# Attention scores for the row maxima: 64 contraction rows instead of 128, heads in pairs, and no transfers that zero the other rows

## The reference, cut to what matters

```
q = apply_rope(proj(Wq))
k = apply_rope(proj(Wk))
v = proj(Wv)
scores = jnp.einsum('bhqd,bhkd->bhqk', q, k) / np.sqrt(HEAD_DIM)
scores = jnp.where(causal[None, None], scores, -jnp.inf)
attn = jax.nn.softmax(scores, axis=-1)
out = jnp.einsum('bhqk,bhkd->bhqd', attn, v)
```

## Time and profile before

| | |
|---|---|
| device time, three runs | 2914.5, 2906.5, 2914.12 us, median 2914.12 |
| the profiled execution, from its first to its last instruction | 2910.5 us |
| time outside that span | not listed for it alone; the median of the runs is 3.6 us above the span |
| PE busy | 2715.2 us, 93% |
| PE weight loads busy | 1717.6 us, 59% |
| DVE, ACT, POOL busy | 1671.6, 1068.5, 928.5 us |
| first attention | about 37 to 430 us of the span |
| in 56 to 430 us of the span: PE, DVE, ACT, POOL busy | 335.62, 254.85, 183.99, 79.54 us of 374.00 |

### The profile page before, as it was taken

One profiled execution on the slowest core, in us unless ns is written; L12 is line 12 of the kernel. 1 busy time (PEld: TensorE's weight loads), 2 busy tenths in 40 slices (PEclk: granted clock), 3 DMA queues, 4 the chain that ended last, 5 costly groups with the idle time before them and its releaser, 6 DMA issues. The chain is left out here.

```text
span 2910.5 us, 35472 instructions
## 1 busy us (share of the span) xinstructions
PE 2715.2 (93%) x13556; PEld 1717.6 (59%) x13556; DVE 1671.6 (57%) x3449; ACT 1068.5 (37%) x1953; POOL 928.5 (32%) x898
## 2 busy tenths in 40 slices
PE   7988989999999999999999999899999999849995
PEld 4445545564656655556555567556666666627983
DVE  6676661217576574575562227688888888433323
ACT  2543551114454453444452115234443444212221
POOL 3222210003232232232220016266666666640004
PEclk8999999989999999999999999899999999869996
DMA  5231301030000000000002000000000000341222
GB/s 181 59 85 46 85 6 59 1 123 20 1 1 1 1 1 1 1 1 1 15 1 101 0 29 1 12 16 12 16 12 16 12 16 16 123 173 39 71 63 87
DMA packets 55961, 108.98 MB, mean 37 GB/s; under 512 B 8128, under 2 KB 32832, under 8 KB 54640
## 3 DMA queue, kind: packets, MB, share of 16 engines
q1 hardware_dynamic: 52720, 98.32, 10.7%
q0 software_dynamic: 3072, 8.39, 0.9%
HBM read 71.10 MB, written 27.00 MB: 34 GB/s over the span
## 5 line engine op out<-in xcount | busy, mean ns | idle before, releaser
L1229 PE MATMUL ps<-back 128*128 128x512 f32 x576 | 292.0, 596 | 0.3 <-ACT back L1270 0.3
L1270 ACT ACTIVATE back<-ps 128x512 f32<-128x512 f32 x288 | 170.0, 597 | 266.4 <-PE ps L1220 264.7
L1265 ACT ACTIVATE back<-ps,front 128x128 f32<-128x128 f32 (+7 forms) x256 | 188.9, 738 | 77.1 <-DVE front L1310 75.3
L1220 PEld LDWEIGHTS ps<-front,back 128*128 128x128 f32 x1152 | 140.8, 141 | 118.2 <-issue 94.8
L1353 POOL TENSOR_TENSOR back<-back 128x512 f32<-128x512 f32 x72 | 91.4, 1269 | 359.5 <-DVE back L1298 359.3
L1363 POOL TENSOR_SCALAR back<-back,front 128x128 f32<-128x128 f32 (+5 forms) x192 | 142.4, 745 | 191.4 <-DVE front L1329 188.6
L1310 DVE TENSOR_REDUCE front<-ps 128x1 f32<-128x128 f32 (+7 forms) x256 | 194.0, 758 | 8.8
L809 ACT ACTIVATE back<-ps 128x1024 f32<-128x1024 f32 (+1 forms) x192 | 150.9, 810 | 128.8 <-PE ps L721 128.2
L1911 DVE TENSOR_TENSOR_SCAN back<-ps,back 128x512 f32<-128x512 f32 x128 | 155.6, 1217 | 43.8 <-PE ps L1728 43.8
L1220 PE MATMUL ps<-front,back 128*128 128x128 f32 x1152 | 170.5, 273 | 3.4 <-DVE back L1335 3.4
L1303 DVE TENSOR_TENSOR ps<-ps,front 128x128 f32<-128x128 f32 x256 | 76.0, 297 | 166.1 <-PE ps L1211 166.1
(11 more groups left out here) (305 smaller groups left out, 5810.5 us busy)
## 6 DMA issues: line engine op xcount, KB each, us to landing
whole<-l_w SPq DMA_DIRECT2D x32, 512.0 KB
front<-back SPq DMA_DIRECT2D x128, 64.0 KB, 2.0
rounded<-qh SPq DMA_DIRECT2D x28, 256.0 KB
rounded<-kh SPq DMA_DIRECT2D x56, 128.0 KB
xg<-front SPq DMA_DIRECT2D x1, 6016.0 KB, 31.8
front<-xg SPq DMA_DIRECT2D x47, 128.0 KB, 2.1
yg<-front SPq DMA_DIRECT2D x47, 128.0 KB, 1.7
front<-l_win SPq DMA_DIRECT2D x1, 4640.0 KB, 17.7
```

What stands on the lines that cost most here:

```text
L1220: t = e.transpose(p[:, h * 128:h * 128 + 128], self.P[n % 2][:, h, j * 128:j * 128 + 128], net.ident)
L1229: e.matmul(PS[:, 7, :], self.V[:, j, G % 4 * 128:G % 4 * 128 + 128], self.turned(("turn", n, j)), start=(j == 0), stop=(j == qt)).then_inc ...
L1265: e.activation(self.P[n % 2][:, h, :nk], s[:, :nk], ACT.Exp, bias=st[:, 0, h:h + 1], scale=1.0, accum_out=st[:, 1, h:h + 1]).then_inc(A.se ...
L1270: e.activation(self.turned(step), self.bank(step), ACT.Copy).then_inc(A.sem, 1)
```

## The change

The matmul of s1 reads only the 64 rows with data. Its steps come in pairs of heads with the same due time; the heads of a pair, 0 with 2 and 1 with 3, have their data in different halves of the rows. The transfers of a set are issued in the order 0, 2, 1, 3, and the ones that zeroed the two extra rows are left out; the count that a waiting matmul asks for falls from 64 to 48 for each set.

```
+    TURNS = (0, 2, 1, 3)
...
-        self.moved = [[net.flag("a_set%d_%d" % (i, h), 48 + 3 * 64) for h in range(4)] for i in range(2)]
+        self.moved = [[net.flag("a_set%d_%d" % (i, h), 48 + 3 * 48) for h in range(4)] for i in range(2)]
...
             if u == 0:
-                s1 = [(t, 0, h) for h in range(4) for t in range(4)]
+                s1 = [(t, 0, h) for a in range(2) for t in range(4) for h in (a, a + 2)]
             else:
-                s1 = [(t, r, h) for t in range(4) for r in range(q + 1) for h in range(4)]
+                s1 = [(t, r, h) for t in range(4) for r in range(q + 1) for h in self.TURNS]
             if pe or dve:
                 for n, s in enumerate(s1):
-                    add(at + reach * (n + 0.5) / len(s1), "s1", u, *s)
+                    add(at + reach * (2 * (n // 2) + 1.0) / len(s1), "s1", u, *s)
...
-            w.wait_ge(self.moved[z % 2][h], 48 + 64 * (z // 2))
+            w.wait_ge(self.moved[z % 2][h], 48 + 48 * (z // 2))
...
-                t = e.matmul(o[:, 0:n], self.QS[:, s, h, qt], self.KS[:, s, h, 512 * r:512 * r + n], start=True, stop=True)
+                rows = slice(64, 128) if h < 2 else slice(0, 64)
+                t = e.matmul(o[:, 0:n], self.QS[rows, s, h, qt], self.KS[rows, s, h, 512 * r:512 * r + n], start=True,
+                             stop=True)
...
-            for h in range(4):
+            for h in self.TURNS:
                 self.move(e, w, z, h, slice(0, 1024), self.moved[s][h])
-                q = self.QS[:, s, h, :].bitcast(F32)
-                e.dma_start(q[32 * h:32 * h + 2, :], q[32 * h + 2:32 * h + 4, :]).then_inc(self.moved[s][h].sem, 16)
```

## The result

The changed kernel takes 2954.71 us (median of four runs, 2941.83 to 2965.86), the kernel before 2914.31 us beside it (four runs, 2906.5 to 2923.2). The ratio is 1.0131, with a 95% interval of 1.0096 to 1.0167: 40 us slower, where 22 to 25 were forecast. The profiled execution is the slowest of the four, 2965.86 us with a span of 2964.1.

What follows compares the result with a forecast made beforehand. TensorE was taken to set the pace in the attention. From the 2910.5 us span, plus 48 for changes of form, minus 34 for overlap, plus 13 for banks, minus 2 swallowed, came 2936 us; range 2900 to 2968.

Steps and rivals of the forecast that it cites:

- 64 rows save nothing by themselves: In s1, a step of 64 rows streams as many columns as one of 128, so nothing is saved.
- Pairs run at once: In s1, the second step of each pair of heads costs nothing, saving 34 us.
- Changes of form, 0.19 us each: On TensorE, switching between 128-row and 64-row steps drains the array and exposes a weight load; 250 changes, 48 us.
- the same holds around pv: At pv's steps, changes of form lengthen the passages too: 0.33 for 0.23 us before, 0.34 for 0.23 behind.
- Banks, 13 us: At s1's three banks, steps wait for VectorE's reads: 9 us in runs of four, 4 after pairs; 0 to 22.
- Swallowed, 2 us: In the attention, some extra work goes into TensorE's 26 us of waits; 2 us taken off.
- the rival "swallowed": In the attention, TensorE's waits shrink as its stream grows: 0 to 8 us more, 2911 to 2919 us; chance 0.13.
- The clock, 0 us: Half-clock stretches, mostly at the turn of units, widen the range some 8 us either way; chance of deciding 0.02.
- The transfers: On SP's queue, 24 issues fewer and the new order count 0, bounds -1 and +2 us.
- the signs that the prediction named: In the timeline after: pair starts under 0.02 us apart, TensorE busy 15 to 25 us longer, s1 waits in runs of four.
- the pairs don't overlap: In s1, second steps save nothing, changes of form still cost 48 us: 2958 us; chance 0.18.
- Faster: At changes of form, a pair's weight load is hidden, 0.08 us per change or less, down to 2889.5 us; chance 0.17.

Runs made afterwards that it cites:

- e3: The kernel before with s1 reading only the 64 rows with data, in the old order, zeroing transfers kept; ratio to before 1.0271.
- e2: The changed kernel with heads 0 and 1, 2 and 3 as pairs, their data in the same half of the rows; ratio to before 1.0226.
- e1: The changed kernel with s1 reading all 128 rows again and the zeroing transfers back, order in pairs kept; ratio to before 1.0057.
- e4: The changed kernel with the 24 zeroing transfers put back and nothing else; ratio to before 1.0120.
- e6: The kernel before with two filling matmuls in each unit's wait for the maxima; ratio to before 0.9982.
- e5: e1 with an extra matmul of 64 rows and 32 columns ahead of each pair; ratio to before 1.0255.
- e11: The changed kernel with VectorE reading only the first 128 columns of every s1 result; ratio to before 1.0004.
- e10: e1 with VectorE reading only the first 128 columns of every s1 result; ratio to before 0.9871.
- e9: The kernel before with VectorE reading only the first 128 columns of every s1 result, for the maxima; ratio to before 0.9855.

## Why the prediction was right, and which of its steps were not

The direction, the main mechanism (changes of form cost more than overlap saves) and the range held. The size was off, 22 to 25 us forecast and 40 measured, and the step most at fault is one that the text set to nothing: "This widens the range by some 8 us either way and decides nothing". That the range held is luck in part: the saving by overlap was counted 12 us too high and the clock at least 23 us too low, but the banks 16 us too high or more, and these errors partly cancel. By its steps:

*64 rows save nothing by themselves.* Right, shown by e3: it is the slowest of all.

*Pairs run at once.* Right in kind, shown by e2 and by the rows above. Mis-sized: the sum counted all second steps, 34 us. 119 of 184 pairs overlap, which by the same prices is 34 x 119/184 = 22 us. The others wait for a bank that VectorE still reads (34.5 us in all, 62 of the 65 released by VectorE). The text had these waits, but added them to a full overlap, which they exclude.

*Changes of form, 0.19 us each.* The price is confirmed row by row (0.10 before, 0.42 instead of 0.23 for the pair, 0.11 behind it). 250 of them are 48 us. The sentence that the same holds around pv is not quite right: the earlier trace rows give 0.10 + 0.09 + 0.11 = 0.30 us for both changes, 0.15 each. Changes into and out of pv stay at 190 in number, so the sum is hardly touched.

*Banks, 13 us.* Mis-sized. s1 steps stand 22.6 us behind the stream after the change (by the count of e1, in which overlapping seconds have none), 25.2 before. The change adds waits through the pairs (e1: 33.7) and takes them away again through its slower issue: -3 us in all.

*Swallowed, 2 us.* The extra waits at s1 that vanish are in the line above. The waits at the maxima fell by 1.7 us, 13.9 to 12.2. Over all steps it was more: banks and swallowed together were put at +11 us, and the waits at full clock fell by 15. This is the mechanism of the rival "swallowed", beside the forecast's own and too small to cancel it.

*The clock, 0 us.* Wrong. Half clock rose by 68.8 us in the attention. At 0.33 us each (e4 against the changed kernel) that is 23 us; counted from all starts it is 31. I took the stretches for a matter of the waits at the maxima, whose number the change leaves alone. They are that in the kernel before (e6), but changes of form add to them (e5, and e11 against e10, where the waits are nearly gone).

The sum so becomes 48 - 22 - 3 + 23 = 46 us, against 43.7 between the last transposes of the maxima, and by the second table 28 - 15 + 31 = 44, where the forecast had 14 + 11 + 0 = 25. For e11 against e10 it is 48 - 26 - 5 + 20 = 37, against 39.1. The rate of 0.33 is from one pair of profiles, so these sums agree within what it can carry and no better. In e5 they don't: its changes and its half clock would be more than 80 us by these prices, and 57 were measured, since 28 us of waits are gone there.

*The transfers.* Right, nothing (e4).

Of the signs that the prediction named, TensorE's busy time grew by 42 us, not 15 to 25, and 65 pairs of 184 start apart. The rest of the program was 10 us longer, which is within what it varies by.

Of the rivals, "the pairs don't overlap" would have come out at about 2958 us, near the measured median, and is still wrong: the trace shows the overlap, and e2 what its absence costs. A median alone would have confirmed it. "Faster" fell since the weight load after a change of form is in the open for pairs as well.

## What to carry to other kernels

Before using row groups for small contractions, count how often the array's form will change and price each at 0.2 us: two steps of 512 columns in one between full-width steps save 0.23 us and cost 0.4. By these prices it pays only where two or more such pairs follow each other, and there the banks must be free; the order here has 23 such places beside 137 lone pairs, and none with more was run. With a ring of three banks 65 of 184 pairs lost their overlap; no run has a larger ring.

Look at the clock's stretches in a stage as a term of the sum. And where an engine empties banks for the bounding one, try shorter reads early: the list of waits named 5 us at s1 and 14 at the maxima, and the experiment gave 42. e9 beats both kernels by 1.4% or more, if the inputs' scores are known to be moderate; e6 is the version that keeps all of the computation, 0.2% faster than before.

## What the runs showed of the hardware

- Steps on 64 rows each, in different halves and to different banks, run at once in this number format: their starts are mostly 0.003 us apart in the records (119 of 184 pairs within 0.03).
- A change between 128-row and 64-row steps costs 0.19 to 0.20 us at the full clock, whichever way. A passage through 32-column steps costs 0.30 us for its two changes.
- TensorE can be busy for 38.45 of 40.96 us at a granted clock of 0.50 all the time (384 to 425 us). With few changes of form and short reads the same unit runs at 1.00: e10 has 4.4 us at half clock up to the last mt, e11 65.5.
- A us at half clock costs less than half a us here: 0.33 us from e4 to the changed kernel, 0.44 over all executions. Steps don't double: a step of 512 columns goes from 0.23 to 0.43 us, a lone pair from 0.42 to 0.73.
